# A graph layer with a gathered x tile in 75 or in all 119 chunks, and GpSimd's gathers in a loop or written out

## The chip, the cores and the metric

The kernel runs on one core of a Trainium2 chip. The metric is the device time of one execution in microseconds; the profile shows one execution on the same core.

## The reference

A graph attention layer, then a small mixture-of-experts layer, each with a layer norm and a residual. There are 12,500 nodes of 256 features and 212,500 edges sorted by their target `dst`.

```python
# graph layer: x normalised row by row, then
h = (x @ W).reshape(n, 4, 64)
a_src = einsum(h, att_src);  a_dst = einsum(h, att_dst)
alpha = leaky_relu(a_src[src] + a_dst[dst], 0.2)
alpha = exp(alpha - segment_max(alpha, dst)[dst])
alpha = alpha / (segment_sum(alpha, dst)[dst] + 1e-16)
out = segment_sum(alpha[:, :, None] * h[src], dst).reshape(n, 256) + bias
x = x + relu(layer_norm(out) * gamma + beta)
# mixture of experts: one routing for the whole batch (from the mean row), the top 2 of 8 experts
x = x + layer_norm(sum_of_two_experts(norm(x)) + norm(x))
```

## The kernel before, in words

**The table stage.** The rows of x are taken in 50 pairs of 128-row blocks. For each pair TensorE transposes the rows (`T*`, L803) and multiplies them with W (`R0`, `R1`, L824), VectorE computes the row statistics, ScalarE scales the product, and SyncE stores 256 rows of `table` in HBM (L516). A table row holds h, ones, and the two logits of a node: 269 numbers.

**The chunk loop.** The edges come in 119 chunks (`chunks`) of 14 tiles of 128 edges. For each chunk GpSimd gathers the table rows of the edges' sources into `rows`, one indirect DMA a tile (L775), into a ring of four buffers. The other engines build one-hot matrices from `dst`, compute the weights, form messages and sum them by target; they work on several chunks at once, each in another part of a step. One step ends one chunk; there are 119 steps and a few around them. ScalarE's `asrc` (L1130) is the first to read a chunk's gathered rows, two steps before its messages are formed. VectorE's `edge_v` (L1429) is the first instruction of a chunk's own step, once per chunk.

**The x tile.** A chunk's last tile (number 13, `GATHERS`) may be had in another way. During the table stage GpSimd gathers the *raw* rows of x for that tile (`gather_x`, L701), for the first `X_CHUNKS` = 75 chunks, and stores them in batches of three gathers to `x_src` in HBM (`store_x`, L718). From batch 12 on, a batch waits for the store three batches back (L707), because it writes where that store's ring has read. In the chunk loop SyncE loads 128 such rows (`xe`, L554), and TensorE, ScalarE and VectorE transpose, normalise and project them (L905, L895, L1162 and others) and so make the 128 table rows themselves. A step of this kind issues 13 gathers, one of the other kind 14. 73 chunks are of the first kind, 46 of the second.

**Order.** All order is written out by hand. Every engine runs `walk` (L435): six steps, then a loop of four steps a round for `X_ROUNDS` = 17 rounds, then a second loop of the other kind up to round `SURE` = 29, then loops that run only if there are more steps (there are none here). On GpSimd four more steps between the two loops are written out. Waits name a point in another engine's list of events (`Ticks`); in a loop the value waited for is in a register. GpSimd's gathers carry no waits: each half step begins with a tiny addition `turn` (L768, L774) that waits in their place, and each x gather with one on `x_turn` (L711). The first wait of a step is for messages of the chunk whose buffer is overwritten and for `expand*`, the second for `lT^` of TensorE. At the table stage's end GpSimd also loads the index tiles of the first four chunks (L737), and SyncE loads what the first steps need: `dst`, windows of the table (L550, L551), and after all stores to `x_src` the first `xe`.

Of the kernel before, what the change touches and what calls it, by code (L numbers as in the profile page):

```python
# [30 lines left out]
P = 128  # L31
# [97 lines left out]
def build(nc, x, src_t, dst, W, att_src, att_dst, g_bias, g_gamma, g_beta, Wr, br, W1, b1, W2, b2,  # L129
# [25 lines left out]
    X_ROUNDS = (3 * PAIRS // 2 - 5) // RING  # L155
    X_CHUNKS = X_ROUNDS * RING + 7
    assert 0 < X_ROUNDS < SURE and X_CHUNKS <= chunks and X_CHUNKS <= 3 * PAIRS // 2 + 2

    with ExitStack() as ctx:
# [9 lines left out]
        x_src = nc.dram_tensor("x_src", [X_CHUNKS * P, D], F32, kind="Internal").ap()  # L169
# [35 lines left out]
        x_turn = sb("x_turn", [1, X_CHUNKS])  # L205
# [99 lines left out]
        x_idx = flat_oh[:, 0:X_CHUNKS * TILES].bitcast(I32)  # L305
        assert 2 * EP <= GATHERS * TW
        x_parts = [slice(i, min(i + X_BATCH, X_CHUNKS)) for i in range(0, X_CHUNKS, X_BATCH)]
# [20 lines left out]
        s_first_idx = sem("s_first_idx")  # L328
# [6 lines left out]
        s_xsrc = [sem(f"s_xsrc{i}") for i in range(RING - 1)]  # L335
        s_xe = [sem(f"s_xe{i}") for i in range(2)]
# [98 lines left out]
        def walk(eng, total, step, long=False, late=0):  # L435
            for j in range(-4, 2):
                step(At(0, RING, j), -j, 5)

            def four(k, late=RING):
                for j in range(RING):  # L440
                    step(At(k, RING, j + 2), -2, 5 if j < late else 2)
# [8 lines left out]
            hold(eng, s_nested)  # L450
            with eng.If(total > SURE * RING + 3):
                with eng.Fori(SURE, (STEPS - 3) // RING, WALK) as far:
                    with eng.If(far * RING + 3 < total):
                        with nc.Fori(far, far + WALK, engines=[eng.engine], hint_back_edge=long) as k:
                            with eng.If(k * RING + 3 < total):
                                four(k, 0)
                        hold(eng, s_nested)

# [11 lines left out]

        def stored_x(eng):
# [5 lines left out]
        def rows_landed(at, lead, hi):  # L477

            if hi > 2:
                return at.landed(GATHERS, lead)  # L480
            return at.landed(TILES, lead) - 16 * len(range(at.slot(lead), X_ROUNDS * RING + 5, RING))

# [7 lines left out]
        def _(sp):  # L490
# [65 lines left out]
            def step(at, lo, hi):  # L556

                before, prev, own, ahead, far, to_row, to_turn, to_load = among(lo, hi)
                if to_load:
# [5 lines left out]
                                                        min_val=0, max_val=X_CHUNKS - 1))  # L565
                if ahead:
                    sp.wait_ge(s_rows[at.slot(1)], rows_landed(at, 1, hi))
# [28 lines left out]
            pairs(SCHED_AT[1], PAIRS // PAIR_RING * PAIR_RING)  # L596
            for at in each_pair(PAIRS // PAIR_RING * PAIR_RING, PAIRS):
# [14 lines left out]
            load_x(0, sp.value_load(step_tab[0:1, 1, 0:1], min_val=0, max_val=X_CHUNKS - 1))  # L612
# [21 lines left out]
            for slot in range(2):  # L634
                sp.wait_ge(s_dst[slot], (total + (2 + 2 - slot)) // 2 * 32)
                hold(sp, s_sp_held)
                sp.wait_ge(s_xe[slot], 16 * len(range(slot, X_CHUNKS, 2)))
# [40 lines left out]
        def _(pool):  # L678
# [18 lines left out]
            def stage(c):  # L697
                c %= x_ring * X_BATCH
                return (c // X_SLOT + 1) * slot_size + c % X_SLOT * D

            def gather_x(c):  # L701
# [13 lines left out]
                if r == X_BATCH - 1 and i > 0:  # L715
                    store_x(i - 1)

            def store_x(i):  # L718
# [4 lines left out]
                pool.dma_start(x_src.rearrange("(q i) d -> q (i d)", i=X_CHUNKS)[:, part.start * D:part.stop * D],  # L723
                               flat_rows[:, bass.ds(stage(part.start), (part.stop - part.start) * D)])\
                    .then_inc(s_xsrc[j], 16)

            pool.wait_ge(s_xidx, 16)
            for c in range(X_CHUNKS // 3):
# [6 lines left out]
            for j in range(RING):  # L735
# [5 lines left out]
            pool.wait_ge(s_first_idx, 16 * RING)  # L741
            for j in range(RING):
                pool.sem_inc(s_idx[j], 16)
# [4 lines left out]
            def gather(at, lo, hi):  # L748
# [14 lines left out]
                if at.off > -1:  # L763
# [1034 lines left out]
```

## Time and profile before

| what | value |
|---|---|
| median of 3 timed runs | 2975.58 us (2974.57 to 2977.32) |
| the profiled execution | 2978.09 us, its span 2976.4 us |
| granted TensorE clock, mean | 0.856 |
| busy: TensorE matmul | 2415.0 us, 81% |
| busy: VectorE | 2279.3 us, 77% |
| busy: ScalarE | 1725.7 us, 58% |
| busy: GpSimd | 1694.2 us, 57% |
| moved by DMA | 417.88 MB, 140 GB/s over the span |

The shares are means over stages that have different limits. GpSimd works in the table stage and the chunk loop alone, so its 57% of the span is far more of those two. An indirect DMA counts as busy on GpSimd while its descriptors are made (957 ns in the mean); the data land later.

### The profile page before, as it was taken

The numbers are of one execution on the slowest core, as the hardware profiler recorded it, in microseconds if no ns is written. First come the engines' busy times: TensorE is split into PE (matmuls) and PEld (weight loads), VectorE is DVE, ScalarE is ACT, GpSimd is POOL, SyncE is SP. The second block draws the span as 40 slices with busy tenths as digits, with TensorE's granted clock in tenths as the row PEclk, the third lists the DMA queues.
The fourth block names the chain that finished last, engine by engine and source line by source line (L and its number), as shares of the span: only waits on it lengthen the run. The fifth ranks groups of instructions, "written<-read, shape, count | busy, mean of one in ns | idle before, by whom it ended". The sixth has DMA issues, their size and how long they took to land. (4 is left out here: it accounts for less than half of the span.)

```text
span 2976.4 us, 67870 instructions
## 1 busy us (share of the span) xinstructions
PE 2415.0 (81%) x13182; PEld 1788.0 (60%) x13182; DVE 2279.3 (77%) x9533; ACT 1725.7 (58%) x5721; POOL 1694.2 (57%) x2041
## 2 busy tenths in 40 slices
PE   7927788888888888887777766777767999999998
PEld 6725566666666666665555555555554666667666
DVE  5638888988989989988888888888875565665655
ACT  4627777777777778777666666666662121221221
POOL 6777777777777777777777777777740000000000
PEclk9959888887878888878777787777778999999999
DMA  8966565656666655665555555555541111101101
GB/s 280 358 180 170 165 174 167 174 167 172 169 170 171 172 168 171 170 169 166 159 162 159 159 156 157 160 160 160 157 113 43 43 36 35 43 29 43 43 28 39
DMA packets 237752, 417.88 MB, mean 140 GB/s; under 512 B 68257, under 2 KB 153121, under 8 KB 237537
## 3 DMA queue, kind: packets, MB, share of 16 engines
q0 software_dynamic: 82640, 239.20, 30.3%
q1 hardware_dynamic: 153546, 175.16, 18.1%
q10 hardware_dynamic: 1351, 1.63, 0.2%
q14 instruction: 200, 1.64, 0.2%
q8 instruction: 15, 0.25, 0.0%
HBM read 362.57 MB, written 53.26 MB: 140 GB/s over the span
## 5 line engine op out<-in xcount | busy, mean ns | idle before, releaser
L775 POOL DMA_INDIRECT rows<-table,idx x1593 | 1524.3, 957 | 448.9 <-issue 386.4
L868 PE MATMUL bank<-msg,oh 128*128 128x260 f32 x3332 | 967.8, 452 | 2.2 <-ACT acc L1144 2.2
L868 PEld LDWEIGHTS bank<-msg,oh 128*128 128x128 f32 x3332 | 757.7, 232 | 147.5 <-DVE r_d L1492 2.6
L1098 ACT ACTIVATE msg<-rows,we 128x65 f32<-128x65 f32 x1904 | 478.5, 333 | 0.4
L916 PE MATMUL bank<-ident_b,ohT 128*128 128x128 bf16 x1680 | 190.0, 300 | 322.3 <-ACT oh L1091 126.5
L1398 DVE TENSOR_TENSOR msg<-rows,bank 128x520 f32<-128x520 f32 x595 | 382.7, 678 | 1.0 <-DVEq L110 0.8
L916 PEld LDWEIGHTS bank<-ident_b,ohT 128*128 128x128 bf16 x1680 | 159.8, 139 | 340.6 <-ACT oh L1091 201.2
L1233 ACT ACTIVATE msg<-bank,b_sb 128x512 f32<-128x512 f32 (+1 forms) x200 | 134.4, 678 | 365.5 <-PE bank L972 347.7
L985 PE MATMUL bank<-rows,msg 128*128 128x256 f32 x1536 | 340.6, 378 | 0.0
L972 PE MATMUL bank<-rows 128*128 128x512 f32 x768 | 335.5, 594 | 4.3 <-DMA rows<-in_L_ffn_W 4.3
L985 PEld LDWEIGHTS bank<-rows,msg 128*128 128x128 f32 x1536 | 288.4, 189 | 51.4 <-issue 10.6
L972 PEld LDWEIGHTS bank<-rows 128*128 128x128 f32 x768 | 146.0, 190 | 179.6 <-issue 175.5
L1118 ACT ACTIVATE carry<-bank 1x265 f32<-1x265 f32 x118 | 45.1, 382 | 311.2 <-PE bank L941 309.5
L1091 ACT ACTIVATE oh_b<-bank 128x896 bf16<-128x896 bf16 x238 | 205.3, 914 | 20.6 <-ACTq L110 15.6
L1091 ACT ACTIVATE oh<-bank 128x896 f32<-128x896 bf16 x238 | 200.7, 890 | 0.3 <-ACTq L110 0.2
L1393 DVE TENSOR_SCALAR ohT<-dst_b,node 128x896 bf16<-128x896 int16 x240 | 161.9, 674 | 8.0 <-DVE mtile L1511 7.4
L1500 DVE TENSOR_REDUCE node_v<-bank 128x70 f32<-128x210 f32 x119 | 44.5, 374 | 157.7 <-PE bank L888 157.5
L1669 DVE TENSOR_TENSOR rows<-bank,msg 128x512 f32<-128x512 f32 x49 | 31.6, 686 | 140.6 <-PE bank L985 137.6
L1180 ACT ACTIVATE selfm<-tab_w,ws 128x65 f32<-128x65 f32 x476 | 127.0, 338 | 3.9
L888 PE MATMUL bank<-ident,asrc 128*70 128x128 f32 x240 | 51.8, 298 | 94.7 <-ACT asrc L1130 78.7
L1148 ACT ACTIVATE r_c<-carry,r_f 1x65 f32<-1x65 f32 x476 | 125.0, 333 | 0.0
L1233 ACT ACT_TABLE_LOAD x12 | 15.4, 1283 | 183.3 <-PE bank L972 183.3
(223 smaller groups left out, 3957.3 us busy)
## 6 DMA issues: line engine op xcount, KB each, us to landing
dst_b<-dst SPq DMA_DIRECT2D x122, 448.0 KB
rows<-table,idx POOLq DMA_INDIRECT x1593
tab_w<-table SPq DMA_DIRECT2D x121, 134.5 KB
x_w<-in_x_rows SPq DMA_DIRECT2D x121, 128.0 KB
x_mid<-x_o SPq DMA_DIRECT2D x119, 128.0 KB
table<-msg SPq DMA_DIRECT2D x50, 269.0 KB, 5.2
rows<-x_mid SPq DMA_DIRECT2D x26, 512.0 KB, 3.5
msg<-in_x_rows SPq DMA_DIRECT2D x51, 256.0 KB
```

The costliest lines, as they stand in the source:

```text
L775: pool.indirect_dma_start(rows[:, slot, t, :], None, table, bass.IndirectOffsetOnAxis(ap=idx[slot][:, t:t + 1], axis=0), bounds_check=None ...
L868: mm = pe.matmul(psA, oh[:, of, t, :], msg[:, of, t, :], start=(t == 0), stop=(t == TILES - 1))
L916: mm = pe.transpose(ps[:, c:c + P], ohT[:, s, t, 0:P], ident_b[:, :])
L972: mm = pe.matmul(u, w1_sb[:, e, k, fk * P:(fk + 1) * P], fxT[:, at.slot(), k, :], start=(k == 0), stop=(k == KD - 1))
L985: mm = pe.matmul(psY[q // 2][:, q % 2, :], hT[:, f, q * P:(q + 1) * P], w2_sb[:, e, fk, :], start=(f == 0), stop=(f == 2 * KF - 1))
L1091: ins = act.activation(to[:, i * half:(i + 1) * half, :], psO[i].rearrange("p (t n) -> p t n", n=P), ACT.Copy)
L1098: ins = act.activation(head_cols(msg[:, s, t, :])[:, h, :], head_cols(rows[:, at.slot(), t, 0:HC1])[:, h, :], ACT.Copy, scale=we[:, t, h:h ...
L1148: ins = act.activation(head_cols(r_c[:, :])[:, h, :], head_cols(carry[:, 0:HC1])[:, h, :], ACT.Copy, scale=r_f[:, h:h + 1])
L1180: ins = act.activation(head_cols(selfm[:, :])[:, h, :], head_cols(tab_w[:, at.slot(), 0:HC1])[:, h, :], ACT.Copy, scale=ws[:, h:h + 1])
L1233: act3.mark(HID[f], act.activation(hT[:, f, 0:n], psU[f % len(psU)][:, 0:n], ACT.Gelu, bias=b1_sb[:, e, fk:fk + 1]))
L1393: return dve.tensor_scalar(ohT[:, s, t, 0:P], dst_b[:, s, :].rearrange("p (t n) -> p t n", n=P)[:, t, :], node[:, s:s + 1], None, ALU.is_e ...
L1398: mark(own, name, lambda: dve.tensor_tensor(msg[:, s, t:t + 2, :].rearrange("p t (h c) -> p t h c", h=H), rows[:, s4, t:t + 2, 0:HC1].rear ...
```

## The change

- `X_CHUNKS` is gone; all 119 chunks have the x tile. The table stage gathers 119 tiles of raw rows instead of 75, at `(c - 2) * PAIRS // chunks` pairs, and `x_src` and its index tile grow in step. Every chunk takes 13 table gathers.
- `walk` has one loop of 29 rounds and one kind of step.
- On GpSimd the chunk loop is written out: 119 steps one after the other, in which the first gather of each half carries the wait itself. The additions `turn` and `x_turn` are gone; `turn` stays only in the loops that do not run here.
- SyncE loads the index tiles of the first four chunks, before the table stage's last two pairs, and stores the last part of `x_src`, two x rows a partition, itself.

```diff
-    X_ROUNDS = (3 * PAIRS // 2 - 5) // RING
-    X_CHUNKS = X_ROUNDS * RING + 7
...
-        def walk(eng, total, step, long=False, late=0):
+        def walk(eng, total, step, long=False):
             for j in range(-4, 2):
                 step(At(0, RING, j), -j, 5)
-            with nc.Fori(0, X_ROUNDS, engines=[eng.engine], hint_back_edge=long) as k:
-                four(k)
-            hold(eng, s_nested)
-            if late:
-                four(X_ROUNDS, late)
-            with nc.Fori(X_ROUNDS + (late > 0), SURE, engines=[eng.engine], hint_back_edge=long) as k:
-                four(k, 0)
+            with nc.Fori(0, SURE, engines=[eng.engine], hint_back_edge=long) as k:
+                four(k, step)
             hold(eng, s_nested)
+            far_rounds(eng, total, step, long)
...
         def stored_x(eng):
             for i in range(RING - 1):
-                eng.wait_ge(s_xsrc[i], 16 * len(x_parts[i::RING - 1]))
+                eng.wait_ge(s_xsrc[i], 16 * len(x_parts[:-1][i::RING - 1]))
                 hold(eng, s_nested)
+            eng.wait_ge(s_xlast, 16)
+            hold(eng, s_nested)
...
+            total = steps_to_run(sp)
+            for j in range(RING):
+                c = sp.value_load(step_tab[0:1, 1, j:j + 1], min_val=0, max_val=chunks - 1)
+                sp.dma_start(idx[j][:, :], src_t[bass.ds(c * P, P), :]).then_inc(s_idx[j], 16)
             for at in each_pair(PAIRS // PAIR_RING * PAIR_RING, PAIRS):
                 pair(at, False)
             store_pair(each_pair(PAIRS - 1, PAIRS)[0], 0)
-            total = steps_to_run(sp)
...
+            for j in range(RING - 1):
+                sp.wait_ge(s_xrow[j], 16 * sum(p.stop - p.start for p in x_parts[j::RING - 1]))
+            sp.dma_start(*x_rows_out(x_parts[-1])).then_inc(s_xlast, 16)
...
                 if c > 1:
-                    pair_of = (c - 2) * 2 // 3
+                    pair_of = (c - 2) * PAIRS // chunks
                     p1_pe.wait(pool, "T*", each_pair(pair_of, pair_of + 1)[0])
-                    pool.tensor_tensor(x_turn[:, c:c + 1], zeros[0:1, 0:1], zeros[0:1, 0:1], ALU.add)
...
-            for c in range(X_CHUNKS // 3, X_CHUNKS - 6):
+            for c in range(chunks // 3, chunks):
                 gather_x(c)
             total = steps_to_run(pool)
-            for j in range(RING):
-                c = pool.value_load(step_tab[0:1, 1, j:j + 1], min_val=0, max_val=chunks - 1)
-                pool.dma_start(idx[j][:, :], src_t[bass.ds(c * P, P), :]).then_inc(s_first_idx, 16)
-            for c in range(X_CHUNKS - 6, X_CHUNKS):
-                gather_x(c)
-            store_x(len(x_parts) - 1)
...
-            def gather(at, lo, hi):
+            def gather(at, lo, hi, repeated=False):
...
-                if at.off > -1:
-                    pool.wait_ge(s_turn, at.k * (2 * RING) + 2 * (at.off + 1))
+                if repeated:
+                    pool.wait_ge(s_turn, at.k * (2 * RING) + 2 * (at.off + 1 - SURE * RING - 2))
                     hold(pool, s_granted)
                 if not first_row:
                     pe2.wait(pool, "expand*", at, -3)
-                pool.tensor_tensor(turn[:, 0:1], turn[:, 2:3], turn[:, 2:3], ALU.add).then_inc(s_turn, 1)
-                n_tiles = GATHERS if hi > 2 else TILES
-                for t in range(n_tiles):
+                if repeated:
+                    pool.tensor_tensor(turn[:, 0:1], turn[:, 2:3], turn[:, 2:3], ALU.add).then_inc(s_turn, 1)
+                for t in range(GATHERS):
...
-            walk(pool, total, gather, late=2)
+            for n in range(-4, SURE * RING + 2):
+                gather(At(0, RING, n), -n if n < 2 else -2, 5)
+            pool.sem_inc(s_turn, 2)
+            far_rounds(pool, total, lambda at, lo, hi: gather(at, lo, hi, repeated=True))
```

GpSimd at the end of the table stage and in the first two chunks, before. `x_src<-rows` is a store of an x batch, `rows<-table,idx` a table gather; `act2`, `dve2` and `pe2` are the event lists of ScalarE, VectorE and TensorE, `s_xsrc` the stores of x rows.

```order
L712 DMA rows<-in_x_rows,oh 128x256
L723 DMA x_src<-rows 128x768 [waits s_xrow2]
L723 DMA x_src<-rows 128x768 [waits s_xrow0]
L768 TENSOR_TENSOR turn<-turn 1x1 [waits s_first_idx,s_dst16,s_tab3,s_idx0,s_tab2,s_tab0,s_tab1]
L775 DMA rows<-table,idx 128x269 x6
L774 TENSOR_TENSOR turn<-turn 1x1
L775 DMA rows<-table,idx 128x269 x7
L768 TENSOR_TENSOR turn<-turn 1x1 [waits s_xsrc0,s_xsrc1,s_xsrc2,s_idx1,act2,dve2,s_turn,pe2]
L775 DMA rows<-table,idx 128x269 x6
L774 TENSOR_TENSOR turn<-turn 1x1 [waits pe2]
L775 DMA rows<-table,idx 128x269 x7
```

The same place in the changed kernel:

```order
L714 DMA rows<-in_x_rows,oh 128x256 [waits p1_pe]
L725 DMA x_src<-rows 128x768 [waits s_xrow2]
L487 TENSOR_LOAD tot_i [waits s_setup]
L487 ISA x2
L767 DMA rows<-table,idx 128x269 [waits s_dst16,s_tab3,s_idx0,s_tab2,s_tab0,s_tab1]
L767 DMA rows<-table,idx 128x269 x12
L767 DMA rows<-table,idx 128x269 [waits s_xsrc0,s_xsrc1,s_xsrc2,s_xlast,s_idx1,act2,dve2,pe2]
L767 DMA rows<-table,idx 128x269 x5
L767 DMA rows<-table,idx 128x269 [waits pe2]
L767 DMA rows<-table,idx 128x269 x6
```

One store of x rows and both additions are gone, and the waits stand on gathers 0 and 6 of a step.

SyncE at the end of the table stage, before: from the second load of `dst` to the first load of x rows (`s_tab`, `s_x`, `s_pad` are stores and loads of the table stage).

```order
L544 DMA dst_b<-dst 128x1792
L549 TENSOR_LOAD step_tab [waits s_x2,s_tab2,s_tab3,s_x1,s_x3,s_tab1,s_pad,s_x0,s_tab0]
L549 ISA x2
L550 ISA
L550 DMA tab_w<-table 128x269
...
L612 TENSOR_LOAD step_tab [waits s_xsrc0,s_xsrc1,s_xsrc2]
L612 ISA x2
L554 ISA
L554 DMA xe<-x_src 128x256
```

And in the changed kernel:

```order
L545 DMA dst_b<-dst16 128x1792
L611 DMA x_src<-rows 128x512 [waits s_xrow2,s_xrow1,s_xrow0]
L550 TENSOR_LOAD step_tab [waits s_x2,s_tab2,s_tab3,s_x1,s_x3,s_tab1,s_pad,s_x0,s_tab0]
L550 ISA x2
L551 ISA
L551 DMA tab_w<-table 128x269
...
L619 TENSOR_LOAD step_tab [waits s_xsrc0,s_xsrc1,s_xsrc2,s_xlast]
L619 ISA x2
L555 ISA
L555 DMA xe<-x_src 128x256
```

The last store of x rows now stands on SyncE, ahead of the eight window loads, and waits there for the last gathered x rows.

## Rows read from the trace of the kernel before

**Rows 1.** windows: busy us of PE, PEld, DVE, ACT, POOL; PEclk, DMA share, GB/s

```profile
0.00:164.00 164.00, 127.08 (x624) 102.31 (x624) 91.15 (x289) 83.86 (x301) 113.64 (x197) 0.94 0.93 316
...
74.00:149.00 75.00, 67.96 (x355) 54.86 (x353) 48.19 (x160) 48.08 (x176) 54.48 (x94) 1.00 1.00 358
149.00:164.00 15.00, 0.84 (x6) 0.25 (x4) 0.00 (x0) 0.71 (x3) 9.23 (x17) 0.61 0.90 285
...
300.00:1300.00 1000.00, 823.76 (x5168) 636.77 (x5168) 894.10 (x3981) 775.28 (x2774) 776.66 (x908) 0.83 0.61 170
```

**Rows 2.** GpSimd's first `turn` in a step: all, 13 gathers, 14, border

```profile
L768 POOL TENSOR_TENSOR turn<-turn x119: 182/183/519, 163.8 to 2172.9; 1x1 f32<-1x1 f32 x119
...
L768 POOL TENSOR_TENSOR turn<-turn x65: 182/183/280, 312.9 to 1372.3; 1x1 f32<-1x1 f32 x65
...
L768 POOL TENSOR_TENSOR turn<-turn x45: 183/229/519, 1389.9 to 2172.9; 1x1 f32<-1x1 f32 x45
...
L768 POOL TENSOR_TENSOR turn<-turn x5: 183/183/272, 1339.2 to 1407.7; 1x1 f32<-1x1 f32 x5
```

**Rows 3.** VectorE's `edge_v`: all, steps 8 to 72, the last but one

```profile
L1429 DVE TENSOR_REDUCE edge_v<-bank x119: 493/500/508, 205.6 to 2225.1; 128x112 f32<-128x336 f32 x119
...
L1429 DVE TENSOR_REDUCE edge_v<-bank x65: 493/500/508, 341.8 to 1404.3; 128x112 f32<-128x336 f32 x65
...
L1429 DVE TENSOR_REDUCE edge_v<-bank x1: 501/501/501, 2205.6 to 2205.6; 128x112 f32<-128x336 f32 x1
```

**Rows 4.** ScalarE's `asrc`: 13 gathers; its wait with 14; the last chunk's

```profile
L1130 ACT ACTIVATE asrc<-rows x63: 247/249/253, 349.3 to 1377.1; 128x70 f32<-128x70 f32 x63
...
  DMA rows<-table,idx: 60.0, 40
...
2196.02 0.27 ACT L1130 ACTIVATE asrc<-rows 128x70 f32<-128x70 f32 x1 [5.47 <-DMA rows<-table,idx]
```

**Rows 5.** timeline, GpSimd, chunk loop: start, us, what, idle before it

```profile
485.39 0.95 POOL L775 DMA_INDIRECT rows<-table,idx  x1 [0.30 <-DVE adsh L1523]
...
486.69 0.96 POOL L775 DMA_INDIRECT rows<-table,idx  x1
```

**Rows 6.** timeline, GpSimd, table stage: first x gather, one batch

```profile
10.65 1.16 POOL L712 DMA_INDIRECT rows<-in_x_rows,oh  x1 [4.47 <-DMA oh<-in_src_tiles]
...
27.34 0.60 POOL L723 DMA_DIRECT2D x_src<-rows  x1
...
28.31 1.01 POOL L712 DMA_INDIRECT rows<-in_x_rows,oh  x1 [0.16 <-issue]
...
31.00 0.97 POOL L712 DMA_INDIRECT rows<-in_x_rows,oh  x1
31.96 0.59 POOL L723 DMA_DIRECT2D x_src<-rows  x1
```

**Rows 7.** the stores to `x_src`, 71 to 142 us, with their landing

```profile
L723 POOL DMA_DIRECT2D x_src<-rows x13: 592/592/594, 73.1 to 136.2; - x13
...
DMA to landing us min/median/max: 5.4/6.4/7.0
```

**Rows 8.** timeline, GpSimd, later in the table stage

```profile
61.44 4.45 POOL L731 TENSOR_SCALAR rows<-rows 128x1666 int16<-128x1666 int32 x1
...
132.53 0.99 POOL L712 DMA_INDIRECT rows<-in_x_rows,oh  x1 [0.47 <-issue]
...
144.39 0.55 POOL L737 DMA_DIRECT2D idx<-in_src_tiles  x1 [1.78 <-issue]
```

**Rows 9.** timeline, SyncE's window and x loads, then ScalarE

```profile
159.82 0.34 SPq L550 DMA_DIRECT2D tab_w<-table  x1
...
167.95 8.61 SPq L554 DMA_DIRECT2D xe<-x_src  x4
...
175.81 0.26 ACT L1164 ACTIVATE rows<-bank,xln 128x4 f32<-128x4 f32 x1
...
182.52 0.27 ACT L1130 ACTIVATE asrc<-rows 128x70 f32<-128x70 f32 x1 [5.40 <-DMA rows<-table,idx]
```

More of the change, by code:

```diff
@@ L168, in build @@
         dst16 = nc.dram_tensor("dst16", [chunks * CHUNK], I16, kind="Internal").ap()
-        x_src = nc.dram_tensor("x_src", [X_CHUNKS * P, D], F32, kind="Internal").ap()
+        x_src = nc.dram_tensor("x_src", [chunks * P, D], F32, kind="Internal").ap()
         x_mid = nc.dram_tensor("x_mid", [XO_ROWS, D], F32, kind="Internal").ap()
@@ L431, in hold, with four, far_rounds @@
             eng.sem_inc(counted, 1)
-        def walk(eng, total, step, long=False, late=0):
-            for j in range(-4, 2):
-                step(At(0, RING, j), -j, 5)
-            def four(k, late=RING):
-                for j in range(RING):
-                    step(At(k, RING, j + 2), -2, 5 if j < late else 2)
-            with nc.Fori(0, X_ROUNDS, engines=[eng.engine], hint_back_edge=long) as k:
-                four(k)
-            hold(eng, s_nested)
-            if late:
-                four(X_ROUNDS, late)
-            with nc.Fori(X_ROUNDS + (late > 0), SURE, engines=[eng.engine], hint_back_edge=long) as k:
-                four(k, 0)
-            hold(eng, s_nested)
+        def four(k, step):
+            for j in range(RING):
+                step(At(k, RING, j + 2), -2, 5)
+        def far_rounds(eng, total, step, long=False):
             with eng.If(total > SURE * RING + 3):
@@ L455, in walk @@
                             with eng.If(k * RING + 3 < total):
-                                four(k, 0)
+                                four(k, step)
                         hold(eng, s_nested)
+        def walk(eng, total, step, long=False):
+            for j in range(-4, 2):
+                step(At(0, RING, j), -j, 5)
+            with nc.Fori(0, SURE, engines=[eng.engine], hint_back_edge=long) as k:
+                four(k, step)
+            hold(eng, s_nested)
+            far_rounds(eng, total, step, long)
         def among(lo, hi):
@@ L469, in each_pair, with stage, x_rows_out, rows_landed @@
             return [At(p // PAIR_RING, PAIR_RING, p % PAIR_RING) for p in range(begin, end)]
+        def stage(c):
+            c %= x_ring * X_BATCH
+            return (c // X_SLOT + 1) * slot_size + c % X_SLOT * D
+        def x_rows_out(part):
+            return (x_src.rearrange("(q i) d -> q (i d)", i=chunks)[:, part.start * D:part.stop * D],
+                    flat_rows[:, bass.ds(stage(part.start), (part.stop - part.start) * D)])
         def stored_x(eng):
             for i in range(RING - 1):
-                eng.wait_ge(s_xsrc[i], 16 * len(x_parts[i::RING - 1]))
+                eng.wait_ge(s_xsrc[i], 16 * len(x_parts[:-1][i::RING - 1]))
                 hold(eng, s_nested)
[L477 to L481, printed above, removed]
+            eng.wait_ge(s_xlast, 16)
+            hold(eng, s_nested)
+        def rows_landed(at, lead):
+            return at.landed(GATHERS, lead)
         def steps_to_run(eng):
@@ L611, in _ @@
             stored_x(sp)
[L612 removed]
+            load_x(0, sp.value_load(step_tab[0:1, 1, 0:1], min_val=0, max_val=chunks - 1))
             walk(sp, total, step)
@@ L636, in _ @@
                 hold(sp, s_sp_held)
-                sp.wait_ge(s_xe[slot], 16 * len(range(slot, X_CHUNKS, 2)))
+                sp.wait_ge(s_xe[slot], (total + (RING + 1 - slot)) // 2 * 16)
                 hold(sp, s_sp_held)
@@ L722, in store_x @@
                 hold(pool, s_granted)
-                pool.dma_start(x_src.rearrange("(q i) d -> q (i d)", i=X_CHUNKS)[:, part.start * D:part.stop * D],
-                               flat_rows[:, bass.ds(stage(part.start), (part.stop - part.start) * D)])\
-                    .then_inc(s_xsrc[j], 16)
+                pool.dma_start(*x_rows_out(part)).then_inc(s_xsrc[j], 16)
             pool.wait_ge(s_xidx, 16)
-            for c in range(X_CHUNKS // 3):
+            for c in range(chunks // 3):
                 gather_x(c)
@@ L784, in _ @@
             hold(pool, s_granted)
-            for t in range(TILES):
+            for t in range(GATHERS):
                 pool.dma_start(spare[0:1, t:t + 1], src_t[0:1, t:t + 1]).then_inc(s_rows[RING - 1], 16)
```

29 lines of the change are left out of this document (11 added, 18 removed).

## The prediction

> **What bounds the kernel now.** I first cut the span into its stages. The table stage lasts until GpSimd's first table gather at 164 us [rows 1, 2], the chunk loop until its last step begins at 2225.1 us [rows 3], and what follows, about 751 us of the 2976.4, is the last step and the feed-forward part, which the change leaves alone.
>
> In the chunk loop two clocks have to be told apart: the pace at which GpSimd issues gathers, and the pace at which the other engines use them up. GpSimd starts a 13-gather step every (1372.3 - 312.9) / 64 = 16.55 us and a 14-gather step every (2172.9 - 1389.9) / 44 = 17.80 us [rows 2]. VectorE's first instruction of a step, which dates the consumers, comes every (1404.3 - 341.8) / 64 = 16.60 us in steps with the x tile [rows 3].
>
> Who waits for whom? ScalarE's `asrc` is the first reader of gathered rows. In the 14-gather stretch it waits for their landing in all 40 steps, 60.0 us in total; in the 13-gather stretch it never waits, in 63 steps [rows 4]. So the last 46 chunks run at GpSimd's pace, 17.8 us. The first 73 run at the consumers' own pace: VectorE is busy for 89% of 300 to 1300 us, and TensorE is granted 0.83 of its clock there [rows 1]. That GpSimd (16.55) and the consumers (16.60) are almost equal there matters below: what GpSimd loses beyond 0.05 us a step shows, and what it gains does not.
>
> **The 46 chunks that get an x tile.** They lose one gather each (1.25 us from start to start [rows 5]) and gain the x tile's work: one 128 KB load, two transposes, two 260-column products, three copies, the statistics. I don't price these one by one, because 64 steps that have all of it show the sum, 16.60 us. From the first `edge_v` on, the loop before takes 2225.1 - 205.6 = 2019.5 us. After, I keep the first 8 steps as they are (341.8 - 205.6 = 136.2; the ring fills), take 109 steps at 16.60 (1809.4) and keep the last one (2225.1 - 2205.6 = 19.5). That makes 1965.1 us, and **-54.4 us** [rows 3]. The step before the last took 21.3 us, 5.5 of them a wait of `asrc` for rows [rows 4]; with the consumers behind GpSimd most of this is covered, and the 109 steps count it so. Bounds: at 16.65 a step -49; with that wait kept -49 too; both, -44.
>
> **Waits on the gathers themselves.** Before, two tiny `turn` instructions in each step carry the waits. A gather, a turn and the next gather take 486.69 - 485.39 = 1.30 us against 1.25 without [rows 5]; with what varies I take 0.08 us each. Without them GpSimd would need some 16.55 - 0.16 = 16.39 us a step. It gains nothing in the loop, since the consumers need 16.60: GpSimd runs ahead until the ring of four is full and then waits. No gather before has its own wait. The nearest rows are the stores to `x_src`, which carry one and start right behind the gather when it is met (31.96 after 31.00 + 0.97 [rows 6]): zero. The upper bound is the gather behind a turn that really waited, idle for 0.47 us where it is 0.16 otherwise [rows 6, 8]: 0.31 us a wait. I take zero, by the store.
>
> **44 more x rows in the table stage.** This is the price. Each is one gather of 128 KB and a third of a 384 KB store. While TensorE's pace or a landed store doesn't hold it, a batch of three gathers and a store takes 31.96 - 27.34 = 4.62 us [rows 6]; without three turns 4.4. From batch 13 on, a batch first waits until the store three batches back has landed. Those take 6.4 us (median) while the DMA engines are full (share 1.00, 358 GB/s), and the batches come every (136.2 - 73.1) / 12 = 5.26 us [rows 1, 7]. Two batches span one landing and one batch: (6.4 + 4.4) / 2 = 5.4, as seen; without turns I take 5.1.
>
> GpSimd's new schedule: start at 10.7 [rows 6] + 1.5 (the index load on ScalarE's queue, for which the first gather waits, grows by 308 KB; at the stage's 316 GB/s [rows 1] that is 1.0, and I take 1.5 since the first loads crowd there) = 12.2. Thirteen batches of 4.4 end at 69.4; the 16-bit conversion takes 4.5 [rows 8], 73.9. TensorE's pairs end at 149 now, where its busy time stops [rows 1]; the 14 or so gathers made earlier bring 3.7 MB more, or 10 us at 358 GB/s, less some 2 us that the engines will use better: 157. Until then (157 - 73.9) / 5.1 = 16.3 batches; the other 10.4, two gathers in the last, take 46 us at 4.4, less 1.3. The last x gather is issued at about 202, and with a store and the load of the step count (1.8 us idle before 144.39 [rows 8]) the first table gather starts near 206. It was 163.8 [rows 2]: **+42 us**. Bounds: no landing ever waited for gives 12.2 + 4.5 + 39.7 x 4.4 = 191 and a start at 195 (+31); 5.4 us a batch to the end gives 217 and a start near 220 (+56).
>
> All this lies on the path. GpSimd is late, and next `asrc`, whose first wait ended with the rows at 182.52, 18.7 us after the first turn [rows 9].
>
> **First loads by SyncE.** GpSimd loses the four index loads with it; before, they began with the 1.78 us ahead of 144.39 [rows 8], and the schedule above has only that load of the step count. SyncE does them ahead of the last two pairs, 40 us before anyone needs them. SyncE also gets the last x store, ahead of eight window loads. Before, its first `xe` load was at 167.95, 4.2 us after the first turn, and the x row was written by 176.1 (175.81 + 0.26 [rows 9]). After, the eight window loads (from 159.82 on, some 7 us) stand behind the last gather's landing, so I count 9 us and then the same 8: ready 17 us after the first gather, against 18.4 for the gathered rows. Hidden, by 1.4 us; without the cover it costs 1 to 4.
>
> **Sum.** -54.4 + 42 = -12.4 us. The profiled execution took 2978.1 us (span 2976.4), so 2965.7; the median of the timed runs lies 2.5 lower, which gives **2963 us**.
>
> A figure that speaks for a cheaper table stage: the Trainium skill (SBUF — State Buffer, Summary: rules for kernel authors) says to reckon with about 358 GB/s between HBM and SBUF, and the trace agrees with 358 GB/s from 74 to 149 us [rows 1]. By that limit alone the 44 rows (11.5 MB in and out) would cost 32 us and the sum would be -22.
>
> **The rivals.**
> 1. *The table stage grows by more.* Stores go on landing late after the pairs are done, since SyncE's broadcast loads take their place. For it: landings of 6.4 us, and DMA share 0.93 over the whole stage [rows 1, 7]. Against: after the pairs GpSimd's own traffic is some 180 GB/s. +50 to +56 gives 2971 to 2982 us.
> 2. *The table stage is bound by bytes alone*, and GpSimd keeps up: +31 to +33, 2952 to 2955 us. Against it: 40 batches at 4.4 us leave no slack.
> 3. *The consumers follow GpSimd.* That 16.55 and 16.60 are so near may be no coincidence; then the pace falls to 16.4 and 109 steps give 20 us more: 2943 us. Against it: `asrc` never waits in those steps.
> 4. *A gather with its own wait is dearer even when the wait is met*: slower than before. At 0.31 us for each of two waits GpSimd's step is 16.39 + 0.62 = 17.01, over the consumers' 16.60; 118 steps take 2007 us against 2172.9 - 163.8 = 2009 now, nothing is won in the loop, and the time is 2976 + 40 = 3016. It decides against the change from 0.14 us a wait on, where 118 steps of 16.67 lose just the 42 us. For it: the 0.47 us. Against: the store's zero.
>
> A branch of rival 4 is that GpSimd's 1,547 gathers in a row, no longer in a loop, stall on the fetch of code. The four steps that were written out before, at the border of the two kinds, kept their pace: from 1339.2 to 1407.7 they take 68.5 us [rows 2], where two steps of each kind make 68.7. So I give it little. The Trainium skill (Runtime: NRT & Kernel Launch, Instruction fetch mechanics) has fetching sequential and hidden, and only taken branches costly; by that rule the change costs nothing here.
>
> **How the numbers follow.** The forecast (2954 to 2971 us) has 0.50, rival 1 0.20, rival 2 0.08, rival 3 0.10, rival 4 0.12. About 0.2% (6 us) is what a measurement of this kernel can tell from no change. Faster than 2969.6 are rivals 2 and 3 and nearly all of the forecast, 0.64; within are rival 1 and the forecast's edge, 0.23; slower is rival 4 and a little of rival 1, 0.13. The range leaves out rival 4 and the far end of rival 3: 2944 to 2984.
>
> **What the new profile would show.** The first table gather near 206 us (195: rival 2; over 214: rival 1). No 17.8 us steps: `edge_v` every 16.6 us to the end. `asrc` without waits for rows. GpSimd waiting for TensorE once or twice a step, by about 0.2 us. Gathers 1.25 us apart with and without a wait (1.5 where one stands: rival 4). If the pace of `edge_v` is 16.4, rival 3 was right. What would make me wrong most easily is the table stage, where my count stacks three estimates: the batch without turns, the landing time under more load, and the end of the pairs.

## The result and the profile after

The changed kernel takes 2971.15 us (median of 20 runs, 2968.83 to 2976.37) against 2976.35 us for the kernel before, run between them: ratio 0.9983, 95% interval [0.9976, 0.9989]. It is faster, by 5.2 us; the forecast was 2963 us, in a range of 2954 to 2971. The profiled execution took 2969.99 us, its span is 2968.2 us, its clock 0.86.

The windows of the profile after, in the columns of [rows 1]:

```profile
10.00:75.00 65.00, 57.07 (x271) 46.12 (x272) 41.32 (x134) 35.49 (x129) 44.61 (x52) 0.97 0.97 332
75.00:146.00 71.00, 65.33 (x341) 52.48 (x340) 47.37 (x154) 45.93 (x168) 48.95 (x53) 1.00 1.01 358
146.00:167.00 21.00, 1.43 (x8) 0.61 (x6) 0.00 (x0) 1.26 (x4) 13.68 (x17) 0.58 0.84 282
167.00:210.00 43.00, 0.00 (x0) 0.00 (x0) 0.00 (x0) 0.00 (x0) 34.11 (x40) 0.50 0.53 180
300.00:1300.00 1000.00, 825.89 (x5191) 638.73 (x5192) 893.85 (x3982) 776.00 (x2777) 754.08 (x788) 0.82 0.61 170
1440.00:2150.00 710.00, 587.36 (x3673) 454.61 (x3673) 634.93 (x2829) 552.40 (x1977) 534.38 (x557) 0.82 0.61 170
```

TensorE's pairs stop near 146 us, but GpSimd goes on alone with x gathers until 210 us, and for 43 us of that no other engine computes. In the chunk loop the last two rows are one picture: VectorE is busy for 89% in both. Before, the second stretch belonged to GpSimd, and VectorE was busy for 82% of it:

```profile
1440.00:2150.00 710.00, 500.49 (x3198) 380.51 (x3198) 582.63 (x2553) 477.08 (x1598) 551.04 (x639) 0.79 0.58 159
```

The groups that date the stages, after (line, count, duration in ns, first and last start; the gathers of the table, those of x, then `edge_v` in all steps, in steps 8 to 72, and from 72 to the last but one, and `asrc` with its only waits for rows):

```profile
L767 POOL DMA_INDIRECT rows<-table,idx x1547: 940/946/1249, 210.5 to 2180.2; - x194
...
L1424 DVE TENSOR_REDUCE edge_v<-bank x119: 493/500/508, 253.0 to 2215.7; 128x112 f32<-128x336 f32 x119
...
L1424 DVE TENSOR_REDUCE edge_v<-bank x65: 493/500/508, 389.6 to 1451.0; 128x112 f32<-128x336 f32 x65
...
L1424 DVE TENSOR_REDUCE edge_v<-bank x46: 495/500/508, 1451.0 to 2197.0; 128x112 f32<-128x336 f32 x46
...
L1125 ACT ACTIVATE asrc<-rows x115: 248/249/268, 296.3 to 2187.7; 128x70 f32<-128x70 f32 x115
...
  DMA rows<-table,idx: 4.2, 3
```

Against [rows 2, 3]: the first table gather is at 210.5 (before, the addition `turn` ahead of it at 163.8 and the gather itself at 164.4), the first `edge_v` at 253.0 (205.6), 47.4 us later. The loop from there to the last `edge_v` takes 2215.7 - 253.0 = 1962.7 us (2019.5), 56.8 us less. Its pace is (1451.0 - 389.6) / 64 = 16.58 us and (2197.0 - 1451.0) / 45 = 16.58 us. What follows takes 752.5 us (751.3). The sum is 47.4 - 56.8 + 1.2 = -8.2 us, the difference of the two spans. The medians differ by 5.2, because the profiled run before was 1.7 us above its median and the one after 1.2 us below. One trace is not exact to a few us: three traces of the kernel before have loops of 2019.5, 2021.0 and 2017.0 us, and a second trace of the changed kernel (2978.85 us, where its median is 2971.02) has its first table gather at 212.4 and a loop of 1969.8 us.

The stores to `x_src` in three stretches, to 75 us, from there to 163, and the rest, each with its landing (us, minimum, median, maximum):

```profile
L725 POOL DMA_DIRECT2D x_src<-rows x12: 578/578/603, 20.9 to 74.3; - x12
...
DMA to landing us min/median/max: 5.4/6.1/7.0
...
L725 POOL DMA_DIRECT2D x_src<-rows x16: 578/580/606, 83.2 to 162.0; - x16
...
DMA to landing us min/median/max: 5.8/6.2/6.9
...
L725 POOL DMA_DIRECT2D x_src<-rows x11: 578/586/598, 166.9 to 209.3; - x11
...
DMA to landing us min/median/max: 2.8/2.8/2.9
```

A batch takes (74.3 - 20.9) / 11 = 4.85 us in the first stretch, (162.0 - 83.2) / 15 = 5.25 us in the second, and 4.36 us once landings have fallen to 2.8 us. GpSimd's waits from 0 to 212 us (who and for what: us in total, times, longest) say why the first two are not 4.36:

```profile
POOL rows L714 <- PE bank L798: 12.6, 17, 1.8
POOL rows L714 <- PE bank L819: 5.9, 16, 1.3
...
POOL rows L714 <- DMA x_src<-rows: 5.2, 5, 1.3
POOL x_src L725 <- DMA rows<-in_x_rows,oh: 5.1, 5, 1.6
```

No single one of them is the price. GpSimd waits for TensorE's pair, for stores to land, and, before a store, for the gathered rows to land.

### The profile page after: what moved, and what is told of

It reads as the page before. It is cut to its first block and busy times, and to the rows that moved or that the text cites. A ratio compares the mean times of both kernels' runs of the same rounds, so it can differ in the third digit from the quotient of the medians.

```text
span 2968.2 us, 68059 instructions
## 1 busy us (share of the span) xinstructions
PE 2475.1 (83%) x13470; PEld 1840.9 (62%) x13470; DVE 2289.9 (77%) x9629; ACT 1770.7 (60%) x6009; POOL 1637.5 (55%) x1737
## 5 line engine op out<-in xcount | busy, mean ns | idle before, releaser
L767 POOL DMA_INDIRECT rows<-table,idx x1547 | 1484.2, 959 | 487.0 <-issue 406.1
L863 PE MATMUL bank<-msg,oh 128*128 128x260 f32 x3332 | 994.2, 462 | 2.6 <-DVEq L110 2.6
L863 PEld LDWEIGHTS bank<-msg,oh 128*128 128x128 f32 x3332 | 775.4, 237 | 156.4 <-DVE r_d L1487 3.0
L714 POOL DMA_INDIRECT rows<-in_x_rows,oh x119 | 114.1, 959 | 55.1 <-issue 21.3
L890 PE MATMUL bank<-wx,xeT 128*128 128x260 f32 x484 | 130.8, 394 | 1.3 <-ACTq L110 1.3
```

The lines of the kernel that those rows point to most:

```text
L767: pool.indirect_dma_start(rows[:, slot, t, :], None, table, bass.IndirectOffsetOnAxis(ap=idx[slot][:, t:t + 1], axis=0), bounds_check=None ...
L863: mm = pe.matmul(psA, oh[:, of, t, :], msg[:, of, t, :], start=(t == 0), stop=(t == TILES - 1))
L890: mm = pe.matmul(psXR, xeT[:, k, :], wx[:, k, 0:D + H], start=(k == 0), stop=(k == KD - 1))
```

## Experiments

Each time is a median beside runs of the kernel before on the same chip; the ratio carries its 95% interval. Paces are from `edge_v`, as above, unless GpSimd's are named.

### Own waits and SyncE's loads, without more x tiles

Against the kernel before, with the x tile still for 75 chunks:

```diff
-                    pool.tensor_tensor(x_turn[:, c:c + 1], zeros[0:1, 0:1], zeros[0:1, 0:1], ALU.add)
...
-            walk(pool, total, gather, late=2)
+            for n in range(-4, SURE * RING + 2):
+                gather(At(0, RING, n), -n if n < 2 else -2, 5 if n < X_ROUNDS * RING + 4 else 2)
...
+                sp.dma_start(idx[j][:, :], src_t[bass.ds(c * P, P), :]).then_inc(s_idx[j], 16)
```

> One part of the change alone: gathers with their own waits, written out, and the first index loads by SyncE, but x tiles for 75 chunks as before. Theory A (the extra x rows are bought too dearly: what the loop wins, about 57 us, the table stage takes back for the most part, and the small savings on GpSimd are what is left): the table stage ends 7 to 10 us earlier (the four index loads and 75 additions are off GpSimd's queue), the 46 steps with 14 gathers go from 17.80 to 17.64 us (-7), the 13-gather steps stay at 16.6; sum -13 to -17 us, 2960 to 2963 us, faster than the full change. Theory B (the x tiles carry the gain, own waits are neutral): no more than -3 us against before, slower than the full change.

Measured: 2969.59 us, ratio 0.9960 [0.9947, 0.9974], where the kernel before took 2981.0. Without a single further x tile this gains more than the whole change (0.9983 [0.9976, 0.9989]). GpSimd sets the pace of the 14-gather steps. Its first gathers of two of them, 44 steps apart:

```profile
1389.74 0.95 POOL L773 DMA_INDIRECT rows<-table,idx  x1 [0.30 <-issue]
...
2164.86 0.95 POOL L773 DMA_INDIRECT rows<-table,idx  x1 [0.30 <-issue]
```

That is (2164.86 - 1389.74) / 44 = 17.62 us a step in place of 17.80 [rows 2], 0.18 us less. This edit takes away two things at once, the additions on `turn` and the loop, but the traces place the gain. In the steps with 14 gathers before, the two stretches from gather to gather that hold an addition are together 0.21 us longer than two without, in the mean; the same two stretches here, 0.02 us. The gain sits where the additions stood. The whole loop, with steps of 16.65 in place of 16.60 in its first part, takes 2011.9 us in place of 2019.5. The first table gather is only 3.4 us earlier (161.0), where 7 to 10 were expected, and the whole gain of 11.4 us is under the expected 13 to 17. The end of the table stage (GpSimd: start, us, what, idle before it):

```profile
152.80 0.58 POOL L727 DMA_DIRECT2D x_src<-rows  x1
159.15 0.57 POOL L727 DMA_DIRECT2D x_src<-rows  x1 [5.78 <-DMA rows<-in_x_rows,oh]
161.01 1.00 POOL L773 DMA_INDIRECT rows<-table,idx  x1 [1.28 <-issue]
```

The last store waits 5.78 us for its own rows with GpSimd's whole queue behind it. That is a price which the changed kernel's last store, on SyncE, avoids.

### The additions put back into the changed kernel's loop

```diff
                 else:
+                    n = 2 * (at.off + 1)
+                    pool.tensor_tensor(turns[:, n:n + 1], zeros[0:1, 0:1], zeros[0:1, 0:1], ALU.add)
```

> The changed kernel with an addition on GpSimd again ahead of gathers 0 and 6 of each step, which takes the waits (without the wait on its own counter). Theory A: GpSimd's free pace goes from 16.4 to 16.55 us a step, still under the consumers' 16.6, so edge_v's pace and the time stay within 3 us. Rival (what GpSimd saves shows): 0.16 us a step, +15 to +19 us.

Measured: 2978.1 us, ratio 0.9992 [0.9983, 1.0001]; in its profile (2973.98 us) the loop takes 1965.5 us, at 16.59 us a step in steps 8 to 72. The pace is that of the changed kernel, so the rival's 15 to 19 us are refuted: where the consumers set the pace, the additions are covered. The intervals of this and of the changed kernel overlap, but a cost of some 3 us over the whole loop is not excluded.

### One table gather fewer a chunk

The changed kernel with 12 table gathers a chunk; tile 12 of every chunk from the fifth on is left out, so old rows stand in its place.

```diff
-                for t in range(GATHERS):
+                for t in range(GATHERS if not repeated and at.off + 1 < RING else GATHERS - 1):
```

> The changed kernel with 12 table gathers a chunk instead of 13 from the fifth chunk on; tile 12's gather is left out and its buffer keeps old rows. Theory A (the loop runs at the consumers' pace): edge_v stays at 16.6 us a step though GpSimd now needs only 15.1; the time moves by less than 3 us. Rival (GpSimd's pace sets the loop, directly or by what its transfers do to the others): up to 1.25 us a step, -100 to -145 us.

```profile
L1424 DVE TENSOR_REDUCE edge_v<-bank x119: 497/500/509, 252.4 to 2219.3; 128x112 f32<-128x336 f32 x119
...
L767 POOL DMA_INDIRECT rows<-table,idx x1432: 940/946/1205, 210.1 to 2181.8; - x179
```

Measured: 2977.2 us, ratio 0.9985 [0.9976, 0.9994]. GpSimd has 115 gathers of 1.25 us less, 144 us of work, and the loop takes 2219.3 - 252.4 = 1966.9 us. The pace from step 8 to 72 is 16.64 us. So GpSimd doesn't set the pace of a step with an x tile, and the consumers don't follow it.

### More semaphores for the x stores

Before a batch GpSimd waits until the store three batches back has landed, since three semaphores serve twelve slots. With twelve of them it is the store twelve batches back:

```diff
-                    pool.wait_ge(s_xsrc[j], 16 * len(range(j, i - 1, RING - 1)))
+                    pool.wait_ge(s_xsrc[i % x_ring], 16 * (i // x_ring))
```

> The changed kernel with 12 semaphores for the stores of x rows instead of 3, so that a batch waits for the store that last used its buffer, 12 batches back, instead of the one 3 back. Theory A (between 75 and 163 us the batches come every 5.25 us because each waits for a landing of some 6.2 us): they come every 4.4 to 4.8 us, the first table gather at 196 to 202 instead of 210.5, and the time falls by 8 to 14 us. Rival (the DMA engines are full, so the gathers' own landings or the pairs take the place of this wait): less than 3 us.

Measured: 2972.97 us, ratio 0.9974 [0.9963, 0.9984]; first table gather 207.4. The middle batches come every 5.01 us in place of 5.25, where 4.4 to 4.8 were expected, and the stage ends 3 us earlier, where 8 to 14 were: the rival was right. The wait has mostly moved: from 84 to 160 us the stores wait 7.9 us in 7 places for gathered rows to land, against 1.5 us in 2. While the DMA engines are full, one landing or another is late.

### One chip on which all these kernels are slower

The next four kernels ran on another chip, on which the kernel before takes 3429.21 us. "sp" means that the last x store is SyncE's, as in the changed kernel; the number is that of the chunks with an x tile.

> The changed kernel once more, as the reference of this call: 0.998 of before, or -5 us. Both theories expect the same.

> 75 x tiles, own waits and first loads by SyncE as in own75, and the last x store on SyncE too, as the full change has it. Theory A (an x tile pays only while its gather lies beside the pairs): GpSimd no longer waits 5.8 us for the last rows before a store; first table gather at 155 us instead of 161, edge_v from 198 to 200 us instead of 203, the rest as in own75: 0.994 to 0.9955 of before, faster than the full change by 8 to 12 us. Rival (the x tiles are what gains): no faster than the full change.

> As own75_sp with x tiles for 87 chunks. Theory A: these 12 tiles are gathered after the pairs at 4.4 us for three (+17 us on the table stage) and save 0.95 us each in the loop (-11): +4 to +8 us against own75_sp. Rival: each tile gains, -3 to -10 us against own75_sp.

> As own75_sp with x tiles for 63 chunks. Theory A: the table stage can't end before the pairs and their stores have landed (near 153 us), so it wins only 0 to 3 us, and 12 more steps run at 17.56 instead of 16.6 us (+11): +8 to +12 us against own75_sp. Rival (the price of an x tile is the same 1.1 us under the pairs as after them): within 3 us of own75_sp.

Measured there: the changed kernel 3541.05 us, ratio 1.0336 [1.0317, 1.0355]; 75 tiles 3495.99, 1.0203 [1.0186, 1.0220]; 87 tiles 3506.42, 1.0230 [1.0206, 1.0253]; 63 tiles 3503.07, 1.0212 [1.0195, 1.0230]. All are slower than before. In the trace of the changed kernel there, `edge_v` (all, then steps 8 to 72) comes every (1808.2 - 440.7) / 64 = 21.37 us. Of SyncE's lines for loads and of a VectorE instruction's waits, from 300 to 1300 us:

```profile
L1424 DVE TENSOR_REDUCE edge_v<-bank x119: 499/501/509, 270.1 to 2782.4; 128x112 f32<-128x336 f32 x119
...
L1424 DVE TENSOR_REDUCE edge_v<-bank x65: 499/501/508, 440.7 to 1808.2; 128x112 f32<-128x336 f32 x65
...
L545 SPq FUSED_REGOPS  x47: 5/47/728, 307.4 to 1292.6; - x47
L545 SPq MOVE dst_b<-dst x47: 5/38/922, 307.5 to 1293.3; - x47
...
L550 SPq SEQ_ASSERT  x46: 5/692/727, 314.6 to 1278.8; - x46
...
L1567 DVE BATCH_NORM_STATS2 st<-o x47: 427/428/428, 308.7 to 1294.1; 128x6 f32<-128x256 f32 x47
...
  remote: 102.6, 40
```

The same lines in the trace of the changed kernel on the first chip:

```profile
L545 SPq FUSED_REGOPS  x61: 43/47/47, 301.7 to 1297.1; - x61
L545 SPq MOVE dst_b<-dst x61: 33/38/38, 301.8 to 1297.2; - x61
...
L550 SPq SEQ_ASSERT  x60: 23/23/23, 308.1 to 1286.4; - x60
```

The work itself is not slower: a gather takes 954 ns there and 959 here, a 128 x 520 product of VectorE 677 ns in both, and the part behind the loop 751.8 us against 752.5. But a register instruction of SyncE that takes 23 to 47 ns elsewhere can take 0.7 us there, and 799 of them do over the span, 318 of these from 300 to 1300 us; none does in the traces of the other chips. VectorE waits 2.6 us, 40 times, at an instruction for which the code has it wait for nothing but its own last result. That these pauses are what makes the loop slow is likely, but no run tests it.

One part of the price can be read. The first and last `edge_v` with 75 x tiles there:

```profile
L1437 DVE TENSOR_REDUCE edge_v<-bank x119: 499/502/508, 224.4 to 2738.0; 128x112 f32<-128x336 f32 x119
```

The loop takes 2513.6 us with 75 x tiles and 2782.4 - 270.1 = 2512.3 with 119. There the 44 further tiles gain nothing in the loop, whose steps take 21.4 us with either number, above both of the usual 16.6 and 17.8, while the stage before it ends 45.7 us later: these are the 45 us between the two kernels. Why the kernel with 75 tiles is still 67 us slower than the kernel before stays open, for lack of a trace of before from that chip.

### The same kernels on the usual chips

> The kernel before, unchanged, so that its trace stands beside the others of this call on the same chip. The experiments of the call before ran on a chip where the kernel before took 3429 us, and where SyncE's register instructions (MOVE, FUSED_REGOPS) took 0.72 or 1.4 us some 490 times in 1000 us, which never happens in the traces of the other chip. If this call lands on such a chip: the theory that those stalls belong to the chip expects them here as well, with a loop some 60 to 100 us shorter than the 2512 of the changed kernel there. If it lands on a chip like the first: 2976 us, loop 2019, ratio 1.000.

> The changed kernel again. On a chip like the first: 0.998 of before, 2971 us, loop 1963. On a chip like the second: 1.034 of before again (a property of the chip and the kernel together, not of one hour), loop 2512.

> x tiles for 75 chunks as before, own waits written out and first loads by SyncE as in the changed kernel, last x store by SyncE. On a chip like the first: own75 gave 0.996 with the last store on GpSimd, which made the first projected rows wait; with the store moved some 2 to 4 us less, 0.9945 to 0.996, faster than the changed kernel. If extending the x tiles to 119 chunks is worth more than it costs, this is slower than the changed kernel (0.998). On a chip like the second: 1.020 again.

> The kernel before with the first index loads alone moved to SyncE; additions on turn and x_turn still carry GpSimd's waits. Theory that the own waits give the gain of own75 (0.996): GpSimd goes on at 17.8 us a chunk with 14 gathers, and only what the first loads take off GpSimd's path (about 5 us between the last x gather and the first table gather) shows: 0.998 to 0.9995. Rival that the loads give most of it: 0.996. On a chip like the second: if this is at 1.00 and own75_sp at 1.02, the own waits and the written-out code cost there; if both are at 1.02, moving the loads to SyncE, whose instructions are slow there, does.

Measured, on one chip: before 2975.77, 0.9998 [0.9989, 1.0007]; the changed kernel 2971.02, 0.9981 [0.9972, 0.9990]; 75 tiles with the last store on SyncE **2962.08, 0.9949 [0.9936, 0.9963]**; before with the first index loads alone moved to SyncE 2972.86, 0.9990 [0.9981, 0.9999]. So of the 14.8 us of the 75-tile kernel SyncE's loads give 3 to 4 us (by the interval, 0.3 to 5.7), and the rest belongs to the own waits, the written-out loop and the last store together. The last store on SyncE brings the first table gather from 161.0 to 157.3 us. The kernels with 75 and with 119 x tiles differ in the number of x tiles and what hangs on it, and on this one chip the 44 further tiles cost 8.9 us.

### How many x tiles

The last group repeats 63 and 87 tiles, and before, on another of the usual chips. The edit is `X_ROUNDS` alone (14, 17, 20).

> The kernel before, for its trace on whichever chip this call gets. On a chip like the one with 3429 us: SyncE's register instructions of 0.72 us here too (some 800 in the span), and a loop 60 to 100 us shorter than the 2512 us of the changed kernel there. On the usual chips: 2976 us, ratio 1.000.

> x tiles for 63 chunks, else as own75_sp (0.9949, 2962 us). Price of an x tile by the trace of own75_sp_again: 12 tiles fewer in the table stage give back 12 times 0 to 1.13 us (nothing where the pairs set the end of the stage, which they do at 143.7 of a last x gather at 147.9), and 12 more chunks at 17.60 in place of 16.63 cost 11.6 us. Theory that tiles gathered while the pairs run are nearly free: slower than own75_sp, some 7 to 11 us, 0.997 to 0.9985. Rival, every tile costs 1.1 us wherever it is: equal to own75_sp, 0.995.

> x tiles for 87 chunks. 12 tiles more, gathered mostly behind the pairs at 4.36 us for three: 12 times 1.13 to 1.45 us is 13.5 to 17.4 us on the stage, 11.6 us back in the loop. Theory: 2 to 6 us slower than own75_sp, 0.9955 to 0.997; the changed kernel's 119 tiles with 0.998 lie on the same line. Rival, more x tiles always pay a little: faster than own75_sp, 0.994.

Measured: before 2980.24, 1.0002 [0.9992, 1.0011]; 63 tiles 2976.02, 0.9986 [0.9977, 0.9995]; 87 tiles 2966.11, 0.9952 [0.9939, 0.9966]. The gathers of x and of the table and the first and last `edge_v`, for 63 tiles:

```profile
L726 POOL DMA_INDIRECT rows<-in_x_rows,oh x63: 940/946/1153, 10.2 to 140.7; - x63
...
L780 POOL DMA_INDIRECT rows<-table,idx x1605: 940/946/1229, 154.7 to 2182.3; - x179
...
L1437 DVE TENSOR_REDUCE edge_v<-bank x119: 495/500/508, 197.8 to 2217.1; 128x112 f32<-128x336 f32 x119
```

for 75:

```profile
L726 POOL DMA_INDIRECT rows<-in_x_rows,oh x75: 940/946/1155, 10.6 to 147.9; - x75
...
L780 POOL DMA_INDIRECT rows<-table,idx x1593: 940/946/1249, 157.3 to 2175.7; - x200
...
L1437 DVE TENSOR_REDUCE edge_v<-bank x119: 493/500/509, 199.4 to 2209.9; 128x112 f32<-128x336 f32 x119
```

and for 87:

```profile
L726 POOL DMA_INDIRECT rows<-in_x_rows,oh x87: 942/946/1154, 10.9 to 164.1; - x87
...
L780 POOL DMA_INDIRECT rows<-table,idx x1581: 940/946/1263, 166.3 to 2175.7; - x198
...
L1437 DVE TENSOR_REDUCE edge_v<-bank x119: 495/502/509, 208.7 to 2211.1; 128x112 f32<-128x336 f32 x119
```

| chunks with an x tile | 63 | 75 | 87 | 119 |
|---|---|---|---|---|
| first table gather, us | 154.7 | 157.3 | 166.3 | 210.5, 212.4 |
| loop, first to last `edge_v`, us | 2019.3 | 2010.5 | 2002.4 | 1962.7, 1969.8 |
| ratio to before | 0.9986 | 0.9949 | 0.9952 | 0.9983, 0.9981 |

TensorE's last products for the pairs begin between 146 and 150 us in all of them. A tile more costs the stage (157.3 - 154.7) / 12 = 0.2 us while GpSimd still ends with the pairs, 0.75 us in the next twelve, and (210.5 - 166.3) / 32 = 1.4 us beyond, where it works alone at 4.36 us for three. The loop gives back 0.7 to 1.2 us a tile all the way, as far as traces whose loops scatter by some us can say. So there is an optimum, and of the four counts tried 75 and 87 are the best. The 2 to 6 us that 87 tiles were expected to lose against 75 are not seen: the two ratios can't be told apart, and they come from two chips. At 119 the additional tiles have eaten three fifths of what the 75-tile kernel gains.

## Why the prediction was right in its parts and wrong in its sum

**The 46 chunks that get an x tile**: right, in mechanism and size. -56.8 us in the profile, -54.4 said; 16.58 us a step to the end, `asrc` without waits after the start. Between the second traces of both kernels it is 2021.0 - 1969.8, or -51.2 us.

**Waits on the gathers themselves**: right, zero. After, in the loop (GpSimd: start, us, what, idle before it):

```profile
498.15 0.95 POOL L767 DMA_INDIRECT rows<-table,idx  x1 [0.30 <-PE bank L900]
499.40 0.95 POOL L767 DMA_INDIRECT rows<-table,idx  x1 [0.30 <-DVE mnode L1520]
```

1.25 us apart, as without a wait [rows 5], and not the 1.5 of rival 4. The prediction also put the two additions at 0.16 us a step, and with 14 gathers 0.18 us went with them. What it didn't ask is what that would be worth in steps that GpSimd paces: the kernel with 75 tiles collects it 46 times, and the changed kernel, with no such steps left, can't.

**44 more x rows in the table stage**: this is the step that failed, by its size. The term was +42 us and is +47.4. It stacked several estimates, and this is how they came out.

The first 39 gathers and 12 stores, up to the conversion, were counted at 4.4 us a batch. They end at 74.9 us and not at 69.4, which is 5.5 us, as much as the whole term missed. The 4.4 came from a batch that met no wait [rows 6]. With more x traffic under the pairs from the beginning, three stores of the first 82 us wait 3.6 us for their rows, a gather 1.2 us for a store, and others up to 0.9 us for a pair. That the additional traffic is what makes these landings late is argued, not tested.

The 80 gathers behind the conversion take 129.0 us, where some 128 were counted. That this came out is in part luck. The prediction let the pairs end at 157 us, delayed by the additional bytes, and the pace fall to 4.4 us from there. But the last products of the pairs begin at 146.4 us (149.7 in the second trace), where before they began at 148.8. Most of the additional bytes found room in the first stretch, where the kernel before left the DMA engines 10% idle: from 10 to 75 us they moved 290 GB/s and now move 332, which is 2.7 MB of the 3.7 (the row of before, then that of the stretch behind the pairs in the changed kernel):

```profile
10.00:75.00 65.00, 56.11 (x265) 46.20 (x266) 41.27 (x131) 34.53 (x126) 45.57 (x70) 0.95 0.90 290
...
148.00:160.00 12.00, 0.15 (x3) 0.04 (x1) 0.00 (x0) 0.00 (x0) 8.50 (x10) 0.55 0.99 319
```

The slow pace went on to 162 us all the same, because the last stores of `table`, zeros for `x_mid` and SyncE's two broadcast loads of `dst` kept the engines at a share of 0.99 until 160. That is the mechanism of rival 1, at a smaller price. From the last x gather to the first table gather, at last, 2.1 us pass, where the prediction left 4, which offsets the rest.

The bound above, 5.4 us to the end and +56, held. By the limit that the prediction quotes from the Trainium skill (SBUF — State Buffer, Summary: rules for kernel authors) the bytes alone would take 32 us, an estimate. The trace has 358 GB/s again from 75 to 146 us, but 180 GB/s from 167 on, where GpSimd's issuing and not the bytes set the time.

**First loads by SyncE**: the projected rows are late, and it shows. They were counted ready 17 us after the first gather, 1.4 us before the gathered ones. After (SyncE, then ScalarE, then GpSimd; start, us, what):

```profile
220.02 9.09 SPq L555 DMA_DIRECT2D xe<-x_src  x4
...
228.36 0.26 ACT L1159 ACTIVATE rows<-bank,xln 128x4 f32<-128x4 f32 x1
...
230.12 0.27 ACT L1125 ACTIVATE asrc<-rows 128x70 f32<-128x70 f32 x1 [0.44 <-ACTq L110]
...
228.47 0.94 POOL L767 DMA_INDIRECT rows<-table,idx  x1 [1.98 <-PEq L110]
```

They are written at 228.6, 18.1 us after the first gather. Before, `asrc` had waited for the gathered rows and started 18.1 us after the first gather (182.52 - 164.4); now it starts 19.6 us after it, and what ended its wait is ScalarE's own queue. GpSimd's first gather of the second chunk waits 2.0 us for TensorE, which itself stood idle until the first `xe` landed; it comes 17.9 us after the first gather, where before it came after 16.5. So the cover was used up, and 1.3 us show: from the first table gather to `edge_v` it is 42.5 us, and was 41.2 (205.6 - 164.4). The prediction counted from the addition ahead of the first gather, 0.6 us earlier, so 0.7 us of the 5.4 that the term missed lie here. What the step did not count either is a gain of GpSimd's: the kernel before with SyncE's loads alone is 3 to 4 us faster (0.9990).

**Sum**: -12.4 us was said, -8.2 measured in the profile, -5.2 in the medians. A sum of two terms near 50 with opposite signs turns an error of 13% in one of them into 4 us of 12. The rest of the way from 2963 to 2971.15 us, 4 us, is no mechanism of the kernel: the forecast took off 2.5 us because the profiled run before lay above the median of three, and the profiled run after lies 1.2 us below its own.

**Rivals.** 1 (stage +50 to +56, 2971 to 2982 us) was the nearest: the first table gather came at 210.5 where 206 and 214 were named, and 2971.15 us lies where the forecast's own range (2954 to 2971) ends and this rival's begins. Its mechanism is there, from 148 to 162 us, though the stage grew by 47.4 and not by 50. 2 (bytes) is refuted by the 43 us in which only GpSimd works. 3 (consumers follow GpSimd) is refuted by the kernel with 12 gathers, 4 by the gathers 1.25 us apart. Its branch, stalls on the fetch of written-out code, shows nowhere: from 300 to 1300 us GpSimd has 681 gaps before a gather that end for no visible reason, and the longest is 0.3 us. By what the prediction quotes from the Trainium skill (Runtime: NRT & Kernel Launch, Instruction fetch mechanics) it costs nothing, and this trace agrees.

## What to carry to other kernels

Work that is moved out of a loop into a stage before it is cheap only while that stage has cover. Count how much of it the cover holds, and stop there: here that was 75 to 87 of 119 tiles. When a change has several parts, price each in the place where its engine sets the pace: the own waits, written out, were worth 0.18 us a step in steps that another part of the change removed. And a price taken from one instance that met no wait is a lower bound, above all where the change raises the traffic around it.

## What the runs showed of the hardware

- A gather with its own semaphore wait follows the one before after 1.25 us, like one without, when the wait is met; with two additions a step as the carriers of the waits, in a loop, a step in which GpSimd sets the pace takes 0.18 us longer (17.80 against 17.62).
- With full DMA engines (share 1.01, 358 GB/s) a 384 KB store lands after 6.2 us; alone with the gathers (0.53, 180 GB/s) it is 2.8 us.
- One chip differed in kind. In four of the five groups of runs the kernel before took 2976 to 2981 us. In one it took 3429 us, with the same durations of work and pauses of 0.7 us in SyncE's and VectorE's own register instructions, and a change that is 0.2 to 0.5% faster elsewhere was 2.0 to 3.4% slower there. There 45 us of the changed kernel's price are its 44 further x tiles; the rest stays open.
